# K projection in front of the output projection in a cross-attention kernel on one core

## The chip, the cores and the metric

The kernel runs on one core of one Trainium2 chip. The metric is the device time of one execution in microseconds (us), and lower is better. Three runs took 1128.15, 1130.78 and 1132.11 us (median 1130.78). A core has a matrix engine (TensorE, PE in the profile), a vector engine (VectorE, DVE), an activation engine (ScalarE, ACT), a general engine (GpSimd, POOL) and a queue that issues the DMAs (SyncE, SP). Each of them works through its own instructions in order; semaphores order them against each other.

## The reference

Eight batch items of 128 tokens with width 512 go through cross-attention with 32 heads of 128, a quantised feed-forward layer, a channel attention with a small convolution, and a routed low-rank layer. The change lies in the attention:

```python
x = _rmsnorm(hidden_states, ln_weight)
h_q = (x @ w_q.T).reshape(b, lq, H, DH)
h_k = (key_value_states @ w_k.T).reshape(b, lk, H, DH)
h_v = (key_value_states @ w_v.T).reshape(b, lk, H, DH)
score = jnp.einsum('bqhd,bkhd->bhqk', h_q, h_k) + position_bias[None]
score = jax.nn.softmax(jnp.where(m, score, -jnp.inf), axis=-1)
attn = jnp.einsum('bhqk,bkhd->bqhd', score, h_v).reshape(b, lq, H * DH)
out = attn @ w_out.T
```

All of it is in float32. A product of two float32 matrices is made of three matmuls: each operand is split into a rounded part ("hi") and the rest ("lo"), and lo by hi, hi by lo and hi by hi are added up.

## The kernel before

**Steps.** The attention is 64 steps, numbered n: 32 heads for batch items 0 to 3 (the first half), then the same heads for items 4 to 7 (the second half). Two steps are a pair, and a pair's odd step also prepares the V weights of a later pair. In the first half VectorE does rounds of a top-k search (`pick_round`) between its attention work; in the second half each step also quantises a slice of the feed-forward weights (`rows=True`).

**TensorE in step n**, in this order (L1273 to L1332): the scores of head n into `pS` (L1282); `queries(n + 1)`, twelve matmuls into `pX0`; `outputs(n - 1)`, twelve matmuls that add attention times W_out into the four banks `oacc`; `keys(n + 1)`, twelve matmuls into `pX1`; the transposes of the probabilities (`pS<-ident,prob`, L1303), which wait for `s_norm_done`; half of `values` of the next pair (24 smaller matmuls); in the second half two small products for the weight slice; then probabilities times V into `pT` (L1331).

**ScalarE in step n** (L624 to L659): four exponentials, the copy of the queries out of `pX0`, `hi("q", n + 2)`, `hi("o", n)`, in the second half the rounding `g_q`, `hi("k", n + 2)`, the copy of the values, in odd steps `value_high`, in the second half two copies (`gu_row`, `wguT`) that count `s_g_out`, then `aT_hi` from `pT`. `hi` rounds a weight tile `raw_*` into `w*_hi`, and first waits until TensorE has finished with the old one: for "o" until `outputs(n - 1)` is done (`s_o_done`), for "k" until `keys(n + 1)` is done.

**GpSimd in step n** (L502 to L513): the masked bias, then `lo("q", n + 2)`, `lo("o", n)`, `lo("k", n + 2)`, in odd steps `lo("v", m + 2)`; each waits for its `hi`.

**SyncE in step n** (L393 to L411): bias n+1, W_q and W_k of n+2, in the second half a slice for the feed-forward weights, W_o of n+1, and in odd steps W_v. There is one buffer `raw_*` of each kind, so a load waits for the `lo` that read the one before: the load of `raw_o` for step n+1 waits for `lo("o", n)`. The load of `raw_v` is issued behind it.

**VectorE in step n** (L891 to L970): `score` (pS plus bias), `neg_max`, in the second half the slice's scale, the pick rounds, the product of `prob` and `row_inv` (L935, sets `s_norm_done`), the copies `k_sb` and `pT_sb`, more pick rounds, then `aT_lo`, which waits for `aT_hi`. The next step's `score` stands behind `aT_lo`.

Of the kernel before, what the change touches and what calls it, by code (L numbers as in the profile page):

```python
# [26 lines left out]
H = 32  # L27
# [22 lines left out]
def layers_kernel(nc, x, cT, mask, bias, ln_w, wq, wk, wv, wo, w_gate, w_up, w_down,  # L50
# [9 lines left out]
    def sem(name):  # L60
        return ctx.enter_context(nc.semaphore(name))

    with ctx:
# [177 lines left out]
        s_g_out = sem("g_out")  # L241
# [73 lines left out]
        def unless_last(n):  # L315

            return not isinstance(n, int) or n < STEPS
# [15 lines left out]
        def later(n):  # L333

            return not isinstance(n, int) or n > 0
# [879 lines left out]
        def _(pe):  # L1215
# [9 lines left out]
            def tr(dst, src, ident):  # L1225
                return mm(dst, src, ident, is_transpose=True, start=True, stop=True)  # L1226
# [13 lines left out]
            def project(dst, c, src, half):  # L1240
                for kt in range(KT):
                    w = tuple(w[c][:, kt * P:(kt + 1) * P] for w in (w_hi, w_lo))
                    last = three(dst, w, tuple(s[half][:, kt, :] for s in src), start=kt == 0, stop=kt == KT - 1)
                return last

            def queries(n, half):
                pe.wait_ge(s_w_lo["q"], n + 1)
                project(pX0[:], "q", (xT_hi, xT_lo), half).then_inc(s_q_proj, 1)

            def keys(n, half):  # L1250
                pe.wait_ge(s_w_lo["k"], n + 1)
                project(pX1[:], "k", (cT_hi, cT_lo), half).then_inc(s_k_proj, 1)

            def values(part, half):

                for i in range(2):
                    b = 2 * part + i
                    for kt in range(KT):
                        c = tuple(t[half][:, kt, b * S:(b + 1) * S] for t in (cT_hi, cT_lo))
                        w = tuple(w["v"][:, kt * 2 * DH:(kt + 1) * 2 * DH] for w in (w_hi, w_lo))  # L1260
                        last = three(pX0[:, i * 2 * DH:(i + 1) * 2 * DH], c, w, start=kt == 0, stop=kt == KT - 1)
                last.then_inc(s_v_proj, 1)

            def outputs(n, start=False):
                pe.wait_ge(s_a_lo, n + 1)
                pe.wait_ge(s_w_lo["o"], n + 1)
                for b in range(HB):
                    cols = slice(b * S, (b + 1) * S)
                    last = three(oacc[b][:], (aT_hi[:, cols], aT_lo[:, cols]), (w_hi["o"][:], w_lo["o"][:]),
                                 start=start, stop=False, lint=True)  # L1270
                last.then_inc(s_o_done, 1)

            def pair(m, half, parity, rows=False):  # L1273
                for odd in range(2):
                    n = 2 * m + odd
                    pe.wait_ge(s_q, n + 1)
                    pe.wait_ge(s_k, n + 1)
                    if later(n):
                        pe.wait_ge(s_pT, n)
                    for b in range(HB):  # L1280
                        cols = slice(b * S, (b + 1) * S)
                        last = mm(pS[:, cols], q_sb[:, cols], k_sb[:, cols], start=True, stop=True)  # L1282
                    last.then_inc(s_s_done, 1)
                    next_half = (n + 1) // H if isinstance(n, int) else half
                    if unless_last(n + 1):
                        if isinstance(n, int) and n + 1 == H:
                            pe.wait_ge(s_xT_lo, B)

                        pe.wait_ge(s_v, n + 2 if not isinstance(n, int) else min(n + 2, STEPS))
                        queries(n + 1, next_half)  # L1290
                    if later(n):
                        if isinstance(n, int) and n == H + 1:
                            pe.wait_ge(s_x1_done, 1)
                        if isinstance(n, int) and n == 1:
                            pe.wait_ge(s_xw, B)
                        outputs(n - 1, start=isinstance(n, int) and n % H == 1)
                    if unless_last(n + 1):
                        if rows and not (isinstance(n, int) and n == H):
                            pe.wait_ge(s_g_out, n - H)
                        keys(n + 1, next_half)  # L1300
                    pe.wait_ge(s_norm_done, n + 1)
                    for b in range(HB):
                        last = tr(pS[:, b * S:(b + 1) * S], prob[:, b, :], ident[:])  # L1303
                    last.then_inc(s_p_trans, 1)
                    if unless_last(n + 2 if odd else n + 3):

                        if isinstance(m, int) and m + 1 == H // 2:
                            pe.wait_ge(s_cT_lo, 2 * KT)
                        pe.wait_ge(s_q, n + 2)
                        pe.wait_ge(s_w_lo["v"], m + 2)  # L1310
                        values(odd, (m + 1) // (H // 2) if isinstance(m, int) else half)
                    if rows:

                        pe.wait_ge(s_g_diag, n - H + 1)

                        if isinstance(n, int) and n + 1 == STEPS:
                            pe.wait_ge(s_g_out, n - H)
                        else:
                            pe.wait_ge(s_k, n + 2)
                        mm(pX1[:, 0:FR], ones[0:FR, :], f_diag[0:FR, 0:FR], start=True, stop=True)  # L1320
                        pe.wait_ge(s_g_q, n - H + 1)
                        for kt in range(KT):
                            last = tr(g_trans_bank[:, kt * FR:(kt + 1) * FR], g_q[0:FR, kt * P:(kt + 1) * P],
                                      ident_b[0:FR, 0:FR])
                        last.then_inc(s_g_trans, 1)
                    pe.wait_ge(s_pT, n + 1)
                    pe.wait_ge(s_v, 2 * m + 2)
                    for b in range(HB):
                        cols = slice(b * S, (b + 1) * S)
                        heads = slice(odd * DH, (odd + 1) * DH)  # L1330
                        last = mm(pT[:, cols], v_sb[parity][:, b, heads], pT_sb[:, cols], start=True, stop=True)  # L1331
                    last.then_inc(s_a_done, 1)  # L1332
# [11 lines left out]
            for m in range(2):  # L1344
                pair(m, 0, m % 2)
            with pe.Fori(1, H // 4 - 1) as u:
                for j in range(2):
                    pair(2 * u + j, 0, j)
            for m in range(H // 2 - 2, H // 2):
                pair(m, 0, m % 2)  # L1350
# [229 lines left out]
```

## Time and profile before

| | |
|---|---|
| Median of three runs | 1130.78 us |
| Profiled execution, own time | 1128.72 us |
| Its span | 1127.0 us |
| Mean granted TensorE clock | 0.96 |
| Busy share PE, PEld, DVE, ACT, POOL | 89%, 76%, 62%, 45%, 44% |
| DMA | 87.22 MB, mean 77 GB/s |

The shares are means over all stages. The attention fills about 57 to 925 us of the span and the rest is what stands before and behind it, so the stage has to be read by itself, in windows and in the order of time. Matmuls overlap: a matmul of 512 columns shows 0.39 us, and the next one starts 0.23 us after it.

### The profile page before, as it was taken

Reading aid. Unit: us, or ns where it says so; the run is one execution under the profiler, and the core shown is the slowest. Engines: PE = TensorE matmul, PEld = TensorE weight load, DVE = VectorE, ACT = ScalarE, POOL = GpSimd, SP = SyncE. Lnnn points to the kernel's source line nnn. Section 1 sums busy time; section 2 is a strip of 40 time slices with the busy share of each in tenths; the row PEclk is TensorE's granted clock in tenths of the full one; section 3 lists DMA queues with packets and bytes.
Section 4 is the critical chain, followed back from the end, with each engine's and each line's share of the span. In section 5 each row is a group of like instructions: output and inputs, shape, how many; then the busy total and the mean of one; then the engine's idle time right before and its main releaser. Section 6 shows DMA issues by size and latency. Waiting matters only on the chain. (4 is left out here: it accounts for less than half of the span.)

```text
span 1127.0 us, 19424 instructions
## 1 busy us (share of the span) xinstructions
PE 1005.8 (89%) x6010; PEld 852.9 (76%) x6010; DVE 697.8 (62%) x1835; ACT 512.3 (45%) x1333; POOL 496.3 (44%) x370
## 2 busy tenths in 40 slices
PE   3798999999999999999999999999999976665455
PEld 2687888888888888888888888888888863332343
DVE  6676777777677677675444444444444479998375
ACT  2334344444434434444444444444444455767342
POOL 4544545454444455434444444444454412554200
PEclk8898999999999999999999999999999999999578
DMA  5222222222222223223222232223223100000001
GB/s 212 75 80 80 80 80 79 79 86 93 88 79 79 79 79 105 80 93 118 94 94 93 94 101 102 102 99 102 92 92 114 58 16 20 1 0 1 0 1 75
DMA packets 50325, 87.22 MB, mean 77 GB/s; under 512 B 6320, under 2 KB 15152, under 8 KB 50288
## 3 DMA queue, kind: packets, MB, share of 16 engines
q1 hardware_dynamic: 50288, 86.76, 23.3%
q8 instruction: 20, 0.33, 0.1%
q14 instruction: 17, 0.14, 0.0%
HBM read 84.64 MB, written 2.10 MB: 77 GB/s over the span
## 5 line engine op out<-in xcount | busy, mean ns | idle before, releaser
L632 ACT ACTIVATE prob<-score,neg_max 128x128 f32<-128x128 f32 x256 | 99.8, 391 | 140.6 <-DVE neg_max L899 140.5
L966 DVE TENSOR_TENSOR aT_lo<-pT,aT_hi 128x512 fp32r<-128x512 f32 x64 | 44.2, 691 | 179.2 <-ACT aT_hi L572 179.1
L1221 PE MATMUL pX<-wv_lo,cT_hi 128*128 128x256 f32 x512 | 151.4, 296 | 0.7 <-ACT v_sb L572 0.7
L464 POOL TENSOR_TENSOR wq_lo<-raw_q,wq_hi 128x512 fp32r<-128x512 f32 x64 | 92.2, 1441 | 130.7 <-ACT wq_hi L572 130.6
L1222 PE MATMUL pX<-wv_hi,cT_lo 128*128 128x256 f32 x512 | 145.9, 285 | 0.0
L1223 PE MATMUL pX<-wv_hi,cT_hi 128*128 128x256 f32 x512 | 145.9, 285 | 0.0
L472 POOL TENSOR_TENSOR b_mask<-b_raw,mask_add 128x512 f32<-128x512 f32 x64 | 74.7, 1168 | 151.2 <-DVE score L896 151.2
L464 POOL TENSOR_TENSOR wv_lo<-raw_v,wv_hi 128x1024 fp32r<-128x1024 f32 x32 | 76.9, 2402 | 109.0 <-ACT wv_hi L572 109.0
L572 ACT ACTIVATE v_sb<-pX 128x512 f32<-128x512 f32 x64 | 38.2, 597 | 175.7 <-PE pX L1223 175.7
L860 DVE COPY k_sb<-pX 128x512 f32<-128x512 f32 x64 | 44.1, 688 | 112.9 <-PE pX L1223 112.9
L1221 PE MATMUL pX<-xT_lo,wq_hi 128*128 128x512 f32 x256 | 107.3, 419 | 4.3 <-DVE xT_lo L848 4.3
L464 POOL TENSOR_TENSOR wk_lo<-raw_k,wk_hi 128x512 fp32r<-128x512 f32 x64 | 83.0, 1297 | 60.8 <-ACT wk_hi L572 60.4
L1221 PE MATMUL oacc<-wo_lo,aT_hi 128*128 128x512 f32 x256 | 100.8, 394 | 6.2 <-DVE aT_lo L966 6.0
L1223 PE MATMUL pX<-xT_hi,wq_hi 128*128 128x512 f32 x256 | 101.4, 396 | 0.0
L1222 PE MATMUL pX<-xT_hi,wq_lo 128*128 128x512 f32 x256 | 100.6, 393 | 0.0
L1222 PE MATMUL oacc<-wo_hi,aT_lo 128*128 128x512 f32 x256 | 100.2, 392 | 0.0
L1223 PE MATMUL oacc<-wo_hi,aT_hi 128*128 128x512 f32 x256 | 100.2, 391 | 0.0
L1221 PEld LDWEIGHTS pX<-wv_lo,cT_hi 128*128 128x128 f32 x512 | 99.3, 194 | 0.9 <-ACT v_sb L572 0.9
L1223 PE MATMUL pX<-cT_hi,wk_hi 128*128 128x512 f32 x256 | 99.8, 390 | 0.0
L1221 PE MATMUL pX<-cT_lo,wk_hi 128*128 128x512 f32 x256 | 99.8, 390 | 0.0
L1222 PE MATMUL pX<-cT_hi,wk_lo 128*128 128x512 f32 x256 | 99.8, 390 | 0.0
L1222 PEld LDWEIGHTS pX<-wv_hi,cT_lo 128*128 128x128 f32 x512 | 99.4, 194 | 0.0
(213 smaller groups left out, 2407.2 us busy)
## 6 DMA issues: line engine op xcount, KB each, us to landing
raw_q<-in_wq SPq DMA_DIRECT2D x64, 256.0 KB, 3.5
raw_k<-in_wk SPq DMA_DIRECT2D x64, 256.0 KB, 3.4
raw_v<-in_wv SPq DMA_DIRECT2D x32, 512.0 KB, 3.9
raw_o<-in_wo SPq DMA_DIRECT2D x64, 256.0 KB, 2.7
b_raw<-in_bias SPq DMA_DIRECT2D x64, 64.0 KB, 3.1
f_raw<-in_w_down SPq DMA_DIRECT2D x4, 688.0 KB, 6.5
g_raw<-in_w_gate SPq DMA_DIRECT2D x16, 172.0 KB
g_raw<-in_w_up SPq DMA_DIRECT2D x16, 172.0 KB
```

The costliest lines, as they stand in the source:

```text
L464: g.tensor_tensor(w_lo[c][:], w_raw[c][:], w_hi[c][:].bitcast(F32), ALU.subtract).then_inc(s_w_lo[c], 1)
L472: g.tensor_tensor(b_mask[:], b_raw[:].to_broadcast([P, HB, S]), mask_add[:, half * HB:(half + 1) * HB, :], ALU.add).then_inc(s_b_mask, 1)
L572: return a.activation(dst, src, ACT.Copy)
L632: e = a.activation(prob[:, b, :], score[:, b, :], ACT.Exp, bias=neg_max[:, b:b + 1], accum_out=row_sum[:, b:b + 1])
L860: v.tensor_copy(k_sb[:], pX1[:]).then_inc(s_k, 1)
L966: v.tensor_tensor(aT_lo[:], pT[:], aT_hi[:].bitcast(F32), ALU.subtract).then_inc(s_a_lo, 1)
L1221: mm(dst, lh, rl, start=start, stop=False, skip_group_check=lint)
L1222: mm(dst, ll, rh, start=False, stop=False, skip_group_check=lint)
L1223: return mm(dst, lh, rh, start=False, stop=stop, skip_group_check=lint)
```

## The change

In each step the twelve matmuls of `keys(n + 1)`, with their waits, are issued in front of those of `outputs(n - 1)`. No instruction is added or removed.

```diff
                         pe.wait_ge(s_v, n + 2 if not isinstance(n, int) else min(n + 2, STEPS))
                         queries(n + 1, next_half)
+                    if unless_last(n + 1):
+                        if rows and not (isinstance(n, int) and n == H):
+                            pe.wait_ge(s_g_out, n - H)
+                        keys(n + 1, next_half)
                     if later(n):
                         if isinstance(n, int) and n == H + 1:
                             pe.wait_ge(s_x1_done, 1)
                         if isinstance(n, int) and n == 1:
                             pe.wait_ge(s_xw, B)
                         outputs(n - 1, start=isinstance(n, int) and n % H == 1)
-                    if unless_last(n + 1):
-                        if rows and not (isinstance(n, int) and n == H):
-                            pe.wait_ge(s_g_out, n - H)
-                        keys(n + 1, next_half)
                     pe.wait_ge(s_norm_done, n + 1)
```

TensorE in a step of the first half before: from the last matmul of the queries (`pX0`) over the output projection (`oacc`) and the K projection (`pX1`) to the transposes.

```order
L1223 MATMUL pX0<-xT0_hi,wq_hi 128x512
L1221 MATMUL oacc0<-wo_lo,aT_hi 128x512 [waits wo_lo,a_lo]
L1222 MATMUL oacc0<-wo_hi,aT_lo 128x512
...
L1223 MATMUL oacc3<-wo_hi,aT_hi 128x512
L1221 MATMUL pX1<-cT0_lo,wk_hi 128x512 [waits wk_lo]
...
L1223 MATMUL pX1<-cT0_hi,wk_hi 128x512
L1226 MATMUL pS<-ident,prob 128x128 [waits norm_done]
```

The same place now:

```order
L1223 MATMUL pX0<-xT0_hi,wq_hi 128x512
L1221 MATMUL pX1<-cT0_lo,wk_hi 128x512 [waits wk_lo]
L1222 MATMUL pX1<-cT0_hi,wk_lo 128x512
...
L1223 MATMUL pX1<-cT0_hi,wk_hi 128x512
L1221 MATMUL oacc0<-wo_lo,aT_hi 128x512 [waits wo_lo,a_lo]
...
L1223 MATMUL oacc3<-wo_hi,aT_hi 128x512
L1226 MATMUL pS<-ident,prob 128x128 [waits norm_done]
```

The K projection moved twelve matmuls forward and the output projection twelve back; the transposes stay where they were.

TensorE in a step of the second half, at the seam in front of the transposes, before:

```order
L1223 MATMUL oacc3<-wo_hi,aT_hi 128x512
L1221 MATMUL pX1<-cT1_lo,wk_hi 128x512 [waits wk_lo,g_out]
L1222 MATMUL pX1<-cT1_hi,wk_lo 128x512
L1223 MATMUL pX1<-cT1_hi,wk_hi 128x512
...
L1226 MATMUL pS<-ident,prob 128x128 [waits norm_done]
```

And now, from the queries on:

```order
L1223 MATMUL pX0<-xT1_hi,wq_hi 128x512
L1221 MATMUL pX1<-cT1_lo,wk_hi 128x512 [waits wk_lo,g_out]
L1222 MATMUL pX1<-cT1_hi,wk_lo 128x512
L1223 MATMUL pX1<-cT1_hi,wk_hi 128x512
...
L1221 MATMUL oacc0<-wo_lo,aT_hi 128x512 [waits wo_lo,a_lo]
```

The wait for `g_out` (the copies of the step before) moved forward with the K projection. The order on VectorE, ScalarE, GpSimd and SyncE is the same before and after.

## Rows read from the trace of the kernel before

**Rows 1.** Stretches: length, busy time of the five, TensorE clock, DMA share, GB/s

```profile
200.00:300.00 100.00, 100.00 (x606) 88.88 (x605) 68.74 (x235) 41.51 (x109) 47.62 (x34) 1.00 0.27 88
600.00:700.00 100.00, 100.00 (x622) 88.90 (x621) 44.76 (x101) 48.47 (x133) 47.57 (x34) 1.00 0.27 88
```

**Rows 2.** TensorE's waits, whole span: total us, times, longest

```profile
PE pS L1226 <- DVE prob L935: 11.0, 7, 3.8
PE oacc L1221 <- DVE aT_lo L966: 6.0, 3, 2.3
```

**Rows 3.** Timeline, odd step 19: ScalarE (start, duration, engine, line, operation)

```profile
315.41 0.63 ACT L572 ACTIVATE wo_hi<-raw_o 128x512 fp32r<-128x512 f32 x1 [1.05 <-PE oacc L1223]
321.87 1.05 ACT L572 ACTIVATE wv_hi<-raw_v 128x1024 fp32r<-128x1024 f32 x1
```

**Rows 4.** Timeline, same step: GpSimd and the DMA issue of SyncE

```profile
316.12 1.29 POOL L464 TENSOR_TENSOR wo_lo<-raw_o,wo_hi 128x512 fp32r<-128x512 f32 x1 [0.39 <-ACT wo_hi L572]
318.94 1.29 POOL L464 TENSOR_TENSOR wk_lo<-raw_k,wk_hi 128x512 fp32r<-128x512 f32 x1 [1.52 <-ACT wk_hi L572]
318.03 0.33 SPq L361 DMA_DIRECT2D raw_v<-in_wv  x1
```

**Rows 5.** Timeline, TensorE in steps 19 and 20

```profile
315.15 0.39 PE L1221 MATMUL pX<-cT_lo,wk_hi 128*128 128x512 f32 x1
317.88 0.38 PE L1226 MATMUL pS<-ident,prob 128*128 128x128 f32 x2
325.73 0.39 PE L1221 MATMUL oacc<-wo_lo,aT_hi 128*128 128x512 f32 x1
331.18 0.27 PE L1226 MATMUL pS<-ident,prob 128*128 128x128 f32 x1
```

**Rows 6.** Timeline, VectorE in steps 19 and 20

```profile
323.44 0.69 DVE L966 TENSOR_TENSOR aT_lo<-pT,aT_hi 128x512 fp32r<-128x512 f32 x1 [2.11 <-ACT aT_hi L572]
328.40 1.72 DVE L935 TENSOR_TENSOR prob<-prob,row_inv 128x512 f32<-128x512 f32 x1
```

**Rows 7.** raw_v, issue to landing, over 120 to 480 us, then 480 to 870

```profile
DMA to landing us min/median/max: 3.3/3.6/4.5
DMA to landing us min/median/max: 3.7/4.1/6.3
```

**Rows 8.** Timeline, steps 23 and 24: a late landing, and the transposes behind

```profile
371.23 0.33 SPq L361 DMA_DIRECT2D raw_v<-in_wv  x1
375.85 1.06 ACT L572 ACTIVATE wv_hi<-raw_v 128x1024 fp32r<-128x1024 f32 x1 [0.66 <-DMA raw_v<-in_wv]
382.37 1.73 DVE L935 TENSOR_TENSOR prob<-prob,row_inv 128x512 f32<-128x512 f32 x1
384.40 0.27 PE L1226 MATMUL pS<-ident,prob 128*128 128x128 f32 x1
```

**Rows 9.** Timeline, TensorE's waits in steps 26, 2 and 33

```profile
411.98 0.33 PE L1226 MATMUL pS<-ident,prob 128*128 128x128 f32 x1 [0.82 <-DVE prob L935]
88.21 0.48 PE L1226 MATMUL pS<-ident,prob 128*128 128x128 f32 x1 [3.79 <-DVE prob L935]
518.25 0.50 PE L1221 MATMUL oacc<-wo_lo,aT_hi 128*128 128x512 f32 x1 [2.34 <-DVE aT_lo L966]
```

**Rows 10.** Timeline, second half, steps 41 and 42

```profile
619.89 0.33 SPq L361 DMA_DIRECT2D raw_v<-in_wv  x1
623.80 1.06 ACT L572 ACTIVATE wv_hi<-raw_v 128x1024 fp32r<-128x1024 f32 x1
630.43 0.69 DVE L935 TENSOR_TENSOR prob<-prob,row_inv 128x512 f32<-128x512 f32 x1
633.44 0.27 PE L1226 MATMUL pS<-ident,prob 128*128 128x128 f32 x1
```

**Rows 11.** Stretches around the idle times of steps 2 and 33, columns as in rows 1

```profile
80.00:90.00 10.00, 6.21 (x29) 5.12 (x28) 8.90 (x23) 3.69 (x12) 8.12 (x7) 0.84 0.00 1
510.00:520.00 10.00, 7.66 (x51) 6.51 (x50) 4.14 (x8) 4.25 (x8) 3.41 (x2) 1.00 0.60 208
```

## The prediction

> **What bounds the kernel now.** I read the stretches first. Over 200 to 300 us and over 600 to 700 us TensorE is busy for the whole 100 us at the full granted clock, VectorE for 69 and 45 us, the others for less than half [rows 1]. So in the attention the time is TensorE's own work, and what the others do costs nothing as long as they are ready in time. The list of TensorE's waits says how rarely they are not: transposes that wait for the softmax product L935, 11.0 us in 7 places, and output projections that wait for `aT_lo`, 6.0 us in 3 [rows 2]. A change of order on an engine that is full can give back no more than such waits. It can cost a lot where it makes somebody else late, so the question is whose work is released by the moved matmuls, and how much room they have.
>
> The timeline of one pair answers that. In odd step 19 the output projection ends where the K projection starts, at 315.15, and the transposes start at 317.88 [rows 5]. `wo_hi` starts 0.26 us after the output projection's end [rows 3], `wo_lo` at 316.12 takes 1.29 us [rows 4], SyncE then issues `raw_o`, and behind it `raw_v` at 318.03 [rows 4]. ScalarE reads `raw_v` at 321.87 (`wv_hi`) [rows 3]. Behind `wv_hi` in ScalarE's queue stands `aT_hi`, for that VectorE waits 2.11 us in front of `aT_lo` at 323.44 [rows 6], and behind `aT_lo` stands all of the next step's softmax, up to L935, which starts at 328.40 and ends at 330.12 [rows 6]. The transposes that need it start at 331.18 [rows 5]. The spare time of this chain is thus 1.06 us.
>
> That the chain is a real one shows where `raw_v` lands late by itself. In step 23 it is read at 375.85, 4.62 us after its issue instead of 3.84; L935 then ends at 384.10 and the transposes start at 384.40, so the spare time shrank from 1.06 to 0.30 us, as much as the read moved [rows 8]. Where GpSimd has one more operation in that place (steps 26 and 28), nothing is left and the transposes wait already [rows 9].
>
> **The change part by part.** It adds and removes no instruction; per step twelve K matmuls move 2.73 us forward (315.15 to 317.88, [rows 5]) and twelve output matmuls as much back. The transposes' place is the same.
>
> K forward. Its weights are ready: `wk_lo` for the next step ends at 320.23 [rows 4], and its matmuls would start where the output projection started, at 325.73 [rows 5], which leaves 5.5 us before and about 4.2 us when `wk_lo` has to go behind `wo_lo` (below). VectorE's `k_sb` comes earlier; it stands between L935 and `pT_sb`, off the tight part. In the second half the wait for the copies (`g_out`) moves forward with it; those copies stand behind `wv_hi` too, but the delay that they bring lies inside the one counted below, since output projection and transposes only follow later. Cost and gain: nothing.
>
> Outputs back, on `aT_lo`: one of the three waits of rows 2 lies in the loop's order, the 2.34 us of step 33 [rows 9]. It goes, since its data is needed 2.73 us later. The other two are at the end of the attention, where no K projection is left. Gain: at most 2.3 us.
>
> Outputs back, on `o_done`: `wo_hi` starts 2.73 us later, and with it `wo_lo`, `raw_o` and `raw_v`, all in odd steps. Four operations in a row on three queues, none with room in it: `wo_hi` waited for TensorE 1.05 us and `wo_lo` for `wo_hi` 0.39 us [rows 3, 4]. `raw_v` is issued at 320.76 instead of 318.03. A landing takes 3.6 us at the median of the first half [rows 7] and about 0.1 us until it is read, so `wv_hi` starts at 324.46, 2.59 us later than before. Everything behind moves as much, as rows 8 show, and against 1.06 us of room (about 0.05 us of it is the semaphore) the transposes of step 20 wait 2.59 - 1.01 = 1.6 us. In even steps no `wv_hi` stands in the queue, so the odd steps' softmax isn't late.
>
> Now the sum. There are 30 odd steps with such a load (n = 1 to 59).
> - First half, ordinary pairs, 11: 11 x 1.6 = 17.6 us.
> - Steps 26 and 28, with no room now: the whole 2.7 us each, 5.4.
> - Second half, 13 pairs: `raw_v` was issued at 619.89 and read at 623.80, L935 ended at 631.12 and the transposes started at 633.44, 2.32 us of room [rows 10]. Issued at 622.62, with the median landing of 4.1 us [rows 7] and 0.1, it is read at 626.82, 3.0 us later; 3.0 - 2.3 = 0.75 us each, 9.8.
> - Steps 2 and 4 have no room either (step 2 waits 3.79 us already [rows 9]): 2.5 each, 5.0.
> - The crossing of the halves: step 32 has no room either, 2.3; step 34 gets the late chain, less the wait that goes in step 33, 1.0 net. Together 3.3.
>
> Sum 41.1 us. The clock comes on top. In step 2 TensorE idled 3.79 us and the granted clock of that stretch of 10 us is 0.84, part of it at the lower of its levels (1.2 instead of 2.4 GHz); around the idle 2.34 us of step 33 it stayed at 1.00 [rows 9, 11]. Steps 2, 4, 26 and 28 would idle over 3 us now. The 0.16 of 10 us is 1.6 us of full speed lost; I take that for two of the four, 3 us, with 0 and 8 as ends. The Trainium skill warns of it in "TensorE: Matmul & The Clock Gate", section "HAM oscillation — how this bites in real kernels": a TensorE that waits for data again and again falls to half its clock each time and pays for warming up again. By that rule the loss would come in all 30 pairs; the trace shows both, a fall behind the longer idle time and none behind the shorter.
>
> From the profiled execution's own 1128.7 us: 1128.7 + 41.1 + 3 = 1172.8. The median of the runs is 2.1 us above it, within their spread of 4 us, so I say 1174.
>
> Bounds. With the shortest landings (3.3 us, [rows 7]) a first-half pair waits 1.3 and one of the second half, whose shortest is 3.7, 0.35: 14.3 + 4.6 + 12.7 for the other places = 31.6, or 1160. With the longest (4.5 us, taken for both halves) it is 2.5 and 1.15: 27.5 + 15 + 14 = 56.5, and 8 us of clock: 1193. A price below nothing is bounded by rows 2: 2.3 us, if nothing of the delay were seen.
>
> **The rivals.**
> *The clock falls in every pair.* The 30 waits leave TensorE idle for 0.7 to 3.7 us (step 2: some 6). If each brought a fall of the size in step 2 (1.6 us in that stretch, and as much again in the next), it would be 30 x 3.2 = 96 us instead of 3: about 1265. For it speaks step 2; against it that 2.34 us of idle time passed without a fall, and that most of the new waits are shorter [rows 9, 11]. Chance 0.05.
> *The delay is covered, and only the wait of step 33 goes (the other side).* The place is `aT_lo` in front of the output projection: the price is minus 2.3 us, 1126.4 on the profiled execution, and 1128.5 against the median. It decides if `wv_hi` comes no more than 1.0 us later, so if SyncE could issue `raw_v` without waiting for `wo_lo`, or if the landing shrank from 3.6 to 2.0 us. Against it: the load stands behind `raw_o` in the order of SyncE, and the shortest landing is 3.3 us. TensorE being full speaks for it only as long as nobody is late. Chance 0.05, most of it within 0.3% of before.
> *Only the first half pays.* If the second half's landings are as short as in step 41 (3.9 us with the read), its term falls to 13 x 0.4 = 5, and without loss of clock the time is 1165. It is inside the range. Chance 0.15, against 0.75 for the forecast.
>
> **How the numbers follow.** The forecast and the last rival make 0.90 and fill 1158 to 1193; I give 1158 to 1192 for 8 in 10, since the places without room (steps 2, 4, 26, 28, 32) are the least certain. 0.3% is 3.4 us, about what runs of this kernel can tell. Slower: 0.75 + 0.15 + 0.05 = 0.95, less 0.01 for what I have not seen: 0.94. Same 0.04, faster 0.02.
>
> **What would show it.** Right, if in odd steps `wo_hi` starts about 0.3 us after the start of the transposes, `raw_v` is issued 2.8 to 2.9 us after it, `wv_hi` starts at 6.4 to 7.5 us instead of 4.0 to 4.8, and if even steps show a wait "pS <- prob L935" of 1.3 to 2.5 us in the first half and 0.4 to 1.2 in the second, some 45 to 55 us in about 30 places instead of 11.0 in 7, while odd steps show none. Even steps would be 14.6 to 15 us long instead of 13.3. The wait of 2.34 us for `aT_lo` in step 33 should be gone. Wrong, if `raw_v` is issued where it was, if L935 ends before the last output matmul all the same, or if the waits fall on odd steps, which would mean that another chain (K's weights) is the late one. A granted clock below 1.00 in the middle of the attention outside steps 24 to 30 would speak for the first rival.

## The result, and the profile after

The changed kernel takes 1166.94 us (median of four runs, 1164.20 to 1169.50) against 1130.24 us for the kernel before in the same comparison: the ratio is 1.0325, with a 95% interval of 1.0294 to 1.0355. It is 36.7 us slower. The forecast was 1174 with a range of 1158 to 1192, by the mechanism that the runs show. Three terms of its sum were two to five times too large, and a part of that was made up by what it had put lower or at nothing.

The page of the changed kernel starts with the span, the busy shares and the TensorE clock in 40 slices:

```profile
span 1162.5 us, 19424 instructions
PE 1018.0 (88%) x6010; PEld 856.4 (74%) x6010; DVE 704.6 (61%) x1835; ACT 508.3 (44%) x1333; POOL 493.1 (42%) x370
PEclk8899899999999999999999999999999998989677
```

The instructions are as many as before and the span is 35.5 us longer. 23.3 us of that are more idle time of TensorE, and its busy time rose from 1005.8 us before to 1018.0, at a mean granted clock of 0.954 instead of 0.964. Its stretches, as in [rows 1] (length, busy times, clock, DMA share, GB/s):

```profile
200.00:300.00 100.00, 94.88 (x565) 83.04 (x565) 70.06 (x228) 39.73 (x106) 46.55 (x33) 1.00 0.25 79
600.00:700.00 100.00, 99.86 (x617) 87.58 (x616) 45.97 (x102) 48.42 (x135) 48.10 (x34) 1.00 0.27 88
```

TensorE was busy for all of both stretches before [rows 1]. Now it idles 5.1% of the first half's stretch, and hardly in the second half's. The list of its waits over the whole span, to be held against [rows 2]:

```profile
PE pS L1226 <- DVE prob L935: 34.9, 18, 5.9
PE oacc L1221 <- DVE aT_lo L966: 3.5, 2, 2.0
PE pX L1221 <- ACT wguT L572: 1.0, 2, 0.8
```

Transposes wait 34.9 us instead of 11.0, in 18 places. The prediction had named 45 to 55 us in about 30 places: in the second half nearly all waits are under 0.15 us, and this list begins there. The 2.34 us in front of the output projection of step 33 are gone, and the two waits at the end of the attention stayed. The third line is the moved wait for `g_out`, in steps 34 and 60. It adds nothing: in both steps the transposes start right behind L935 all the same, 0.05 to 0.06 us after its end.

Now the chain, in steps 17 and 18, for [rows 3 to 6]. First ScalarE, GpSimd and SyncE, then VectorE, then TensorE (start, duration, operation, idle time before it and its releaser):

```profile
306.02 0.63 ACT L572 ACTIVATE wo_hi<-raw_o 128x512 fp32r<-128x512 f32 x1 [3.78 <-PE oacc L1223]
306.73 1.30 POOL L464 TENSOR_TENSOR wo_lo<-raw_o,wo_hi 128x512 fp32r<-128x512 f32 x1 [3.12 <-ACT wo_hi L572]
308.63 0.33 SPq L361 DMA_DIRECT2D raw_v<-in_wv  x1
312.19 1.06 ACT L572 ACTIVATE wv_hi<-raw_v 128x1024 fp32r<-128x1024 f32 x1 [2.33 <-DMA raw_v<-in_wv]
313.77 0.69 DVE L966 TENSOR_TENSOR aT_lo<-pT,aT_hi 128x512 fp32r<-128x512 f32 x1 [4.27 <-ACT aT_hi L572]
318.71 1.71 DVE L935 TENSOR_TENSOR prob<-prob,row_inv 128x512 f32<-128x512 f32 x1
...
305.76 0.60 PE L1226 MATMUL pS<-ident,prob 128*128 128x128 f32 x4
320.47 0.33 PE L1226 MATMUL pS<-ident,prob 128*128 128x128 f32 x1 [1.25 <-DVE prob L935]
```

From the start of the transposes (305.76) it is 0.26 us to `wo_hi`, 2.87 to `raw_v`'s issue, 6.43 to its reading (before: 0.15 and 3.99, [rows 3 to 5]). ScalarE, which did not wait for this DMA in step 17 before, waits 2.33 us for it, and step 18 is 14.71 us long instead of 13.30.

In the second half, steps 41 and 42, for [rows 10]:

```profile
650.50 0.33 SPq L361 DMA_DIRECT2D raw_v<-in_wv  x1
654.16 1.06 ACT L572 ACTIVATE wv_hi<-raw_v 128x1024 fp32r<-128x1024 f32 x1 [2.45 <-DMA raw_v<-in_wv]
660.79 0.69 DVE L935 TENSOR_TENSOR prob<-prob,row_inv 128x512 f32<-128x512 f32 x1
661.54 0.33 PE L1226 MATMUL pS<-ident,prob 128*128 128x128 f32 x1
```

L935 ends at 661.48 and the transposes start 0.06 us later, so all 2.3 us of room are used, and 0.2 us more. Landings of `raw_v`, for [rows 7] (120 to 480 us, then 480 to 870):

```profile
DMA to landing us min/median/max: 3.3/3.4/4.3
DMA to landing us min/median/max: 3.5/3.5/4.3
```

### The profile page after: what moved, and what is told of

It is laid out like the page before. It is cut to its first block and busy times, and to the rows that moved or that the text cites. A ratio compares the mean times of both kernels' runs of the same rounds, so it can differ in the third digit from the quotient of the medians.

```text
span 1162.5 us, 19424 instructions
## 1 busy us (share of the span) xinstructions
PE 1018.0 (88%) x6010; PEld 856.4 (74%) x6010; DVE 704.6 (61%) x1835; ACT 508.3 (44%) x1333; POOL 493.1 (42%) x370
## 5 line engine op out<-in xcount | busy, mean ns | idle before, releaser
L464 POOL TENSOR_TENSOR wo_lo<-raw_o,wo_hi 128x512 fp32r<-128x512 f32 x64 | 86.9, 1358 | 104.7 <-ACT wo_hi L572 104.6
L572 ACT ACTIVATE wo_hi<-raw_o 128x512 fp32r<-128x512 f32 x64 | 40.4, 631 | 137.8 <-PE oacc L1223 137.7
L1223 PEld LDWEIGHTS pX<-wv_hi,cT_hi 128*128 128x128 f32 x512 | 100.5, 196 | 0.0
```

What stands on the lines that cost most here:

```text
L464: g.tensor_tensor(w_lo[c][:], w_raw[c][:], w_hi[c][:].bitcast(F32), ALU.subtract).then_inc(s_w_lo[c], 1)
L572: return a.activation(dst, src, ACT.Copy)
L1223: return mm(dst, lh, rh, start=False, stop=stop, skip_group_check=lint)
```

## The experiments

Theory A: `outputs` behind `keys` lets `wo_hi` start 2.7 us later; `wo_lo`, `raw_o` and, in SyncE's order, `raw_v` follow; `wv_hi` stands in front of `aT_hi` in ScalarE's queue, and `aT_lo` in front of the next softmax on VectorE. Rival B: the moved K projection costs by itself (its weights, the wait for `g_out`, GpSimd and VectorE in each other's way). Times of the kernel before, in the first set of four, have a median of 1129.59 us, in the second of three 1129.55.

**The load of W_v first.** The changed kernel, SyncE's order alone edited:

```diff
+                    if odd and unless_last(n + 3):
+                        load("v", m + 2, ...)
                     if unless_last(n + 1):
                         load("o", n + 1, head1)
-                    if odd and unless_last(n + 3):
-                        load("v", m + 2, ...)
```

> The changed kernel (K projection first), with one edit: in the odd steps SyncE issues raw_v in front of raw_o, so that it no longer stands behind a load that waits for wo_lo. Theory A (the loss is the late raw_v, which holds up wv_hi, aT_hi, aT_lo and the next softmax): wv_hi starts again right behind v_sb, 4.0 us after the start of the transposes instead of 6.4, aT_lo at 5.6 instead of 8.0, and the waits of the transposes in the middle of the first half are gone (steps of 13.30 us); the output projection's 2.3 us wait for aT_lo in step 33 is gone too. Time 1124 to 1131 us. Rival B (the moved K projection costs by itself, through wk_lo behind wo_lo, the moved wait for g_out, or GpSimd and VectorE in each other's way): little changes, 1155 to 1167 us.

Measured: 1123.52 us, ratio 0.9945 (0.9927 to 0.9963). All of the loss is gone and 6 us more, 0.5 us below the 1124 to 1131 expected. The chain in steps 15 to 17 (SyncE, ScalarE, VectorE, and TensorE's transposes of step 17) and the remaining waits of the attention:

```profile
280.75 0.33 SPq L361 DMA_DIRECT2D raw_v<-in_wv  x1
293.48 1.05 ACT L572 ACTIVATE wv_hi<-raw_v 128x1024 fp32r<-128x1024 f32 x1
295.05 0.69 DVE L966 TENSOR_TENSOR aT_lo<-pT,aT_hi 128x512 fp32r<-128x512 f32 x1 [1.83 <-ACT aT_hi L572]
289.48 0.27 PE L1226 MATMUL pS<-ident,prob 128*128 128x128 f32 x1
...
PE pS L1226 <- DVE prob L935: 8.3, 4, 3.5
PE oacc L1221 <- DVE aT_lo L966: 3.5, 2, 2.0
```

`raw_v` is issued 8.73 us ahead of the transposes and read 4.00 us behind them, with `wo_hi` as late as in the changed kernel. Rival B falls: with K first and every other consequence of it in place, nothing is lost. The 6 us come mostly from places where the kernel before waits or its clock is low: in the profiled attention step 34 is 2.6 us shorter than in the kernel before, steps 26 to 29 together 2.1 and steps 3 and 4 together 2.0, while step 1 is 1.5 us longer, by a fall of the clock.

**The same edit on the kernel before.**

> The kernel before (output projection first), with the same edit of SyncE alone. Theory A: the loads that landed late (read 4.6 to 4.8 us after the transposes' start) are early now, so steps 4, 26 and 28 lose most of their waits of 1 us and step 33 its 2.3 us: 2 to 5 us faster than before, 1125 to 1129 us, and within 2 us of the same edit on the changed kernel. Rival B: also about 1126, but then the same edit on the changed kernel stays 30 us above it.

Measured: 1128.17 us, ratio 0.9977 (0.9963 to 0.9991). It is faster than before by 0.2%, but 4.7 us slower than the same edit with K first, not within 2 us as expected. The intervals of the two ratios touch at 0.9963, but all six runs of the one (1123.20 to 1125.06 us) are faster than all twelve of the other (1125.70 to 1129.14), so once the load is early the kernel with K first is the faster one. In the profiled attention (from the transposes of step 0 to those of step 63) the two differ by 2.4 us (855.8 and 853.4), mostly in steps 4, 33, 26 and 28. The other 2.5 us of the two profiles lie outside the attention, where the kernels are the same (taken up below), so only about half of the difference is explained by the order. The 2.6 us in step 34 come here as well: that gain belongs to the early load and needs no move on TensorE.

**`wo_hi` late by itself.** The kernel before, TensorE untouched:

```diff
+                    if unless_last(n + 1):
+                        act.wait_ge(s_k_proj, n + 2)
                     hi("o", n, s_o_done)
```

> The kernel before, TensorE's order untouched; ScalarE's rounding of W_o (wo_hi) waits in addition until the K projection of the step is done, as it has to in the changed kernel by the order. Theory A: the whole loss comes back without any move on TensorE: wo_hi at 0.26 us after the transposes' start, raw_v issued at 2.9, wv_hi at 6.4, waits of about 1.3 us in the even steps of the first half; time 1162 to 1170 us. The wait for aT_lo in front of the output projection may come in addition, since aT_lo at 8.0 us is later than the 7.85 us at which the output projection starts. Rival B: the time stays at 1130 to 1135 us, since TensorE does what it did.

Measured: 1177.44 us, ratio 1.0402 (1.0373 to 1.0432). The loss comes without any move on TensorE, and 10 us more of it than in the changed kernel, above the 1162 to 1170 expected. TensorE's waits in the attention (up to 925 us), then the chain in step 17 (transposes at 303.37; the lines of the kernel are two higher here):

```profile
PE oacc L1223 <- DVE aT_lo L968: 31.1, 30, 2.0
PE pS L1228 <- DVE prob L937: 11.3, 16, 4.9
...
303.70 0.63 ACT L572 ACTIVATE wo_hi<-raw_o 128x512 fp32r<-128x512 f32 x1 [3.85 <-PE pX L1225]
306.31 0.33 SPq L361 DMA_DIRECT2D raw_v<-in_wv  x1
310.99 1.06 ACT L572 ACTIVATE wv_hi<-raw_v 128x1024 fp32r<-128x1024 f32 x1 [3.52 <-DMA raw_v<-in_wv]
```

The offsets are nearly those of the changed kernel, 0.33 and 2.94 us for 0.26 and 2.87. The output projection now stands first and meets the late `aT_lo` in all 30 pairs, in the second half too, where the softmax has room. So K first both makes the delay and shields TensorE from a part of it: of the 48 us that a late `wo_hi` costs with the old order, 37 are left with the new one.

**`wv_hi` behind `aT_hi`.** The changed kernel, ScalarE's order alone edited: `value_high(m + 2)` moves to the line after the copy into `aT_hi`.

> The changed kernel, with one edit on ScalarE: in odd steps the rounding of W_v (wv_hi) stands behind aT_hi instead of in front of it; raw_v is issued as late as in the changed kernel. Theory A (the link from raw_v to the softmax is ScalarE's queue): aT_lo starts at 5.0 us after the transposes' start, the second half has no waits. In the first half wv_lo (2.4 us on GpSimd) now falls beside the pick copies L924 and may hold them up by 1 to 2 us, as cT_lo does in step 26, so some wait of 0 to 1 us can stay there: 1126 to 1145 us. If instead the late raw_v harms in another way (wv_lo late for the values), it stays at 1155 or more.

Measured: 1126.71 us, ratio 0.9976 (0.9959 to 0.9994). `raw_v` is issued 2.87 us behind the transposes and read at 6.2 to 7.8, as late as in the changed kernel, yet `aT_lo` starts at 5.02 (5.43 in the second half) and the loss is gone. The link is ScalarE's queue. Where waits would be left I had the halves the wrong way round: the first half has none in its ordinary pairs, the second has mostly 0.2 to 0.5 us of room left and waits in five steps (34, 36, 54, 58 and 60). What takes the room is GpSimd, here in steps 41 and 42 (GpSimd, then VectorE):

```profile
621.37 2.40 POOL L464 TENSOR_TENSOR wv_lo<-raw_v,wv_hi 128x1024 fp32r<-128x1024 f32 x1 [4.04 <-ACT wv_hi L572]
623.73 1.16 POOL L472 TENSOR_TENSOR b_mask<-b_raw,mask_add 128x512 f32<-128x512 f32 x1
...
621.49 0.68 DVE L904 TENSOR_REDUCE f_s<-g_raw 86x1 f32<-86x512 f32 x1 [0.17 <-issue]
622.58 1.24 DVE L911 TENSOR_SCALAR f_diag<-ident,f_s 86x86 f32<-86x86 f32 x1
623.92 1.25 DVE L917 TENSOR_SCALAR g_mag<-g_raw,f_s 86x512 f32<-86x512 f32 x1
625.33 1.01 DVE L932 TENSOR_TENSOR row_inv<-row_inv,row_any 128x4 f32<-128x4 f32 x1
```

`wv_lo` now runs beside the softmax. L911 shows 1.24 us where it took 0.26 in the kernel before, L917 1.25 instead of 0.48, L932 1.01 instead of 0.16, while the reduction L904 keeps its 0.68.

**Both edits.**

> The changed kernel with both edits: raw_v issued in front of raw_o, and wv_hi behind aT_hi in ScalarE's queue. Theory A says that either edit alone takes raw_v out of the softmax's chain, so the second brings little: wv_hi at 5.5 us and aT_lo at 5.0 us after the transposes' start instead of 5.6, half a us less wait in steps 2 and 32, 1121 to 1125 us. Theory C (GpSimd's wv_lo now falls beside VectorE's next softmax and holds its copies and products up, as in the second half of the run with wv_hi behind aT_hi alone): nothing gained or 1 to 3 us lost against the early load alone, 1123 to 1127 us.

Measured: 1127.36 us, ratio 0.9999 (0.9983 to 1.0015). Theory C was right that the second edit does harm beside the first: 4 us more than the early load alone, where it had said 1 to 3. Two thirds of the harm are at one place. `wv_hi` now comes at 4.9 instead of 4.0 us, and GpSimd's `wv_lo` and the four `xT_lo` end 14.1 us behind the transposes of step 1 instead of 13.2. GpSimd's next operations then run beside the end of VectorE's softmax: L924 takes 2.01 us instead of 0.91 and L935 1.67 instead of 0.69. Step 2 is 18.99 us long instead of 16.97, and the clock falls for 6.8 us there instead of 3.4. Steps 4 and 32 add 0.6 us each.

**Second half only.** The load order of the first experiment, in the second half alone.

> The changed kernel; raw_v is issued in front of raw_o in the second half alone, and stays behind it in the first. This splits the loss by half. By the trace of the changed kernel the second half's 13 pairs lost 4.3 us and the late chain of steps 33 and 34 little: 1160 to 1163 us. By the prediction's own term (9.8 us for these pairs): 1155 to 1158 us. If the loss were even over the pairs it would be near 1147 us.

Measured: 1164.0 us, ratio 1.0293 (1.0258 to 1.0329), 1155.85 to 1173.44 over four runs. The first half holds nearly all of the loss. For the numbers of the two sides (1160 to 1163 and 1155 to 1158 us) the runs spread too far to decide; an even spread over the pairs (1147) is out. The spread itself tells something. The clock of the longest execution (1173.44 us) in three stretches is

```profile
280.00:320.00 40.00, 37.86 (x225) 33.74 (x224) 23.42 (x80) 12.60 (x32) 16.39 (x12) 0.96 0.25 80
430.00:490.00 60.00, 53.66 (x294) 47.22 (x293) 38.61 (x118) 20.62 (x56) 25.83 (x19) 0.91 0.27 86
600.00:900.00 300.00, 300.00 (x1888) 267.57 (x1887) 129.07 (x283) 139.81 (x379) 142.62 (x99) 1.00 0.31 95
```

In the first two stretches the clock falls three times, at waits of 2.14, 2.67 and 3.67 us (steps 16, 26 and 28), and it stays up at the waits of 1.2 to 1.9 us in the other steps from 6 to 24. So with waits in every pair the granted clock can drop in the middle of the attention, and without them, in the second half, TensorE is busy for 300 of 300 us at full clock.

**The early load, and `add_norm` early.** On top of the first experiment, VectorE does `add_norm` of steps 1 and 31 in front of its wait for `aT_hi`:

```diff
+                    if isinstance(n, int) and n in (1, H - 1):
+                        add_norm(n // (H - 1))
                     dve.wait_ge(s_a_hi, n + 1)
                     v.tensor_tensor(aT_lo[:], pT[:], aT_hi[:].bitcast(F32), ALU.subtract)
-                    if isinstance(n, int) and n in (1, H - 1):
-                        add_norm(n // (H - 1))
```

> The changed kernel with raw_v issued in front of raw_o, and in steps 1 and 31 VectorE does add_norm (four operations on xr that the attention doesn't need) in front of its wait for aT_hi instead of behind aT_lo. In step 1 VectorE idles there for about 2.5 us, and GpSimd isn't working beside it. If the remaining waits of steps 2 and 32 come from add_norm standing in front of the next softmax, step 2 gets 3 to 4 us shorter, the clock doesn't fall behind it, step 32 loses its 0.4 us: 1117 to 1121 us. If they come from the late aT_hi or from GpSimd, it stays at 1123 us.

Measured: 1122.53 us, ratio 0.9944 (0.9926 to 0.9963). VectorE in step 1, first with the early load alone, then with this edit:

```profile
77.08 0.69 DVE L966 TENSOR_TENSOR aT_lo<-pT,aT_hi 128x512 fp32r<-128x512 f32 x1 [1.83 <-ACT aT_hi L572]
77.87 5.75 DVE L855 TENSOR_SCALAR xr<-xr,keep,shift 128x512 f32<-128x512 f32 x4
```

```profile
75.47 4.01 DVE L855 TENSOR_SCALAR xr<-xr,keep,shift 128x512 f32<-128x512 f32 x4
79.39 0.68 DVE L968 TENSOR_TENSOR aT_lo<-pT,aT_hi 128x512 fp32r<-128x512 f32 x1
```

Step 2 gets 1.3 us shorter (15.67 for 16.97) and step 32 loses its 0.4 us, less than the 3 to 4 us expected: `wv_lo` on GpSimd starts at 76.77 here, so `add_norm` isn't alone after all. And the softmax is held up instead, beside GpSimd's work: L924, L932 and L935 of step 2 take 1.57, 0.90 and 1.68 us where they took 0.91, 0.16 and 0.69 with the early load alone. The clock still falls behind step 2. Against the early load alone the time can't be told apart (1122.53 and 1123.52 us, with nearly the same interval); the two are the fastest versions here.

## Why the prediction was right, and which terms were off

**The chain** came as forecast, link by link: `wo_hi` 0.26 us after the transposes' start, `raw_v` issued at 2.87, read at 6.3 to 7.3 in the first half, and waits for L935 in even steps of it (odd steps stay at 13.37 us). Cutting it at SyncE or at ScalarE removes the loss, making `wo_hi` late by itself brings it, there mostly as waits for `aT_lo`.

**The terms**, from the step lengths of the two profiled executions:

| term | forecast | measured |
|---|---|---|
| 11 ordinary pairs, first half | 17.6 | 17.4 |
| steps 26 and 28 | 5.4 | 1.1 |
| 13 pairs, second half | 9.8 | 4.3 |
| steps 2 and 4, waits | 5.0 | 4.7 |
| crossing, without clock | 3.3 | 0.7 |
| clock | 3 | 4.0 |
| outside the attention | 0 | 3.5 |
| sum | 44.1 | 35.7 |

The spans differ by 35.5 us; the remaining steps make up -0.2. The forecast was 8.4 us too high, and that is a balance: the first five terms are 12.9 us too high together, the last two 4.5 us too low. So the closeness of the total is in part luck. That the mechanism was right shows in the first term and in the chain.

*Second half.* The term mis-sized most is this one, by the landing of 4.1 us: here it was 3.5 at the median, and a wait is what is left of the delay after 2.3 us of room, so 0.6 us less landing turns 0.75 us of wait into 0.15 to 0.25. Where one landing was long (step 59, read at 7.65 us) the next step got 1.34 us longer. 0.8 of the 4.3 us are in the odd steps, each 13.77 us long instead of 13.70, which I had not counted. I had taken the landing time from the place where the kernel before issues `raw_v`. The three profiled executions that issue it 2.7 us later (this one, only `wo_hi` late, and `wv_hi` behind `aT_hi`) all have a median of 3.5 us in the second half, against 4.1 in the kernel before. Whether the median belongs to the place of the issue or to the execution stays open, with one profile of the earlier place. The long landings differ between executions: with only `wo_hi` late the second-half reads are spread from 6.3 to 7.6 us, here they lie at 6.4 to 6.6 but for step 59 and step 33. So this term depends on the execution too, and the profiled one was the fastest of the four runs of the changed kernel (1164.20 us). I took a median where room minus delay was near zero; the rival "only the first half pays" had the better number for this term, 5 us. Its total of 1165 is close by the same balance, since it too had 5.4 us for steps 26 and 28 and no clock.

*Steps 26 and 28.* The term, "the whole 2.7 us each", took L935 of before as fixed. It wasn't; VectorE, then GpSimd, in step 26 before and after:

```profile
406.27 2.18 DVE L924 TENSOR_SCALAR pick<-cT_raw 128x128 f32 x2 [0.19 <-issue]
410.23 1.69 DVE L935 TENSOR_TENSOR prob<-prob,row_inv 128x512 f32<-128x512 f32 x1
410.09 1.29 POOL L464 TENSOR_TENSOR wo_lo<-raw_o,wo_hi 128x512 fp32r<-128x512 f32 x1
```

```profile
429.08 2.16 DVE L924 TENSOR_SCALAR pick<-cT_raw 128x128 f32 x2 [0.19 <-issue]
433.03 0.69 DVE L935 TENSOR_TENSOR prob<-prob,row_inv 128x512 f32<-128x512 f32 x1
433.23 1.63 POOL L464 TENSOR_TENSOR wo_lo<-raw_o,wo_hi 128x512 fp32r<-128x512 f32 x1 [0.29 <-ACT wo_hi L572]
```

L935 started beside GpSimd's `wq_lo` and `wo_lo` before; now `wo_hi` comes later, GpSimd has a gap of 0.29 us, L935 starts in it, 0.20 us ahead of `wo_lo`, and takes 0.69 us. That is 1.0 us per step in favour of the change, by a narrow margin: in the profile of "second half only", with the same order in the first half and `raw_v` read 0.26 us later, L935 of step 26 starts 0.04 us behind `wo_lo` and takes 1.76 us. The landings of these two pairs were also 1.1 to 1.2 us shorter than in the profile before (3.3 and 3.4 us against 4.5).

*Crossing.* Step 32 got 3.0 us longer, step 33 2.2 (the clock took 2.6 us there, and the 0.5 us went by which step 33 was longer than an ordinary step before), and step 34 2.0 shorter. There the landing of 6.3 us of the profile before was 4.3.

*Clock.* I charged two new falls; two came, behind step 4 and behind step 32. The stretches with them, and TensorE's idle times in front:

```profile
120.00:130.00 10.00, 8.95 (x50) 8.73 (x51) 6.79 (x23) 1.20 (x2) 2.12 (x2) 0.67 0.29 87
520.00:530.00 10.00, 9.89 (x58) 9.59 (x59) 5.96 (x10) 4.13 (x8) 3.67 (x3) 0.70 0.29 103
...
121.05 0.47 PE L1226 MATMUL pS<-ident,prob 128*128 128x128 f32 x1 [3.41 <-DVE prob L935]
520.11 0.48 PE L1226 MATMUL pS<-ident,prob 128*128 128x128 f32 x1 [3.27 <-DVE prob L935]
```

A fall costs 2.5 us here; the 4.0 us of the table are 2.5 in step 5 and 2.6 in step 33, less 1.1 in step 3, behind whose start both kernels have a fall (granted clock over 90 to 95 us 0.63 before, 0.75 after), the changed kernel's more of it in TensorE's idle time. Behind waits of 1.2 to 2.1 us the clock stayed at 1.00 in this execution; the rival in which each pair falls was wrong as a rule. The length of the wait alone doesn't decide in these profiles: 2.34 us (kernel before) and 2.12 us (changed kernel) passed without a fall, and the 3.17 us in front of step 0's transposes passed in both kernels but not with the early load, while the clock fell at 2.11 us (`wv_hi` behind `aT_hi`), 2.14 us (second half only) and 2.22 us (`add_norm` early), and at 1.98 and 1.79 us with only `wo_hi` late. The Trainium skill's "TensorE: Matmul & The Clock Gate", section "HAM oscillation — how this bites in real kernels", describes a kernel in which TensorE waits for a DMA longer than it works, time after time. Here it works for most of each pair, and the prediction's reading that by that rule all 30 pairs would fall goes beyond the page. The traces bear it out for the longest waits and for some of the shorter ones.

*Outside the attention* nothing was forecast and 3.5 us were measured, 0.8 less ahead of it and 4.3 more behind. I don't put that down to the change: the same part is 267.4 us long in the kernel before, 270.9 in the changed one, 268.1 with the early load, 270.7 with the early load on the old order and 266.8 in the last experiment (273.0 at most, with the second half only), with nothing edited there and the clock at its lower level in other places each time. That it is the clock's place is argued, not tested.

**The gain** of 2.3 us at step 33 came, hidden under the loss, but not by the move alone. The landing there was 2.0 us shorter, and `aT_lo` started 9.05 us behind the transposes instead of 10.01; the early load brings the gain with the old order too. The other side failed as its condition said: the delay of `wv_hi` was 2.4 us, not below 1.0.

## What to carry to other kernels

Where the engine is busy all the time, as here, a swap of two pieces of work is decided by who waits for the piece that moves back, through all the queues behind it; here the path was TensorE, ScalarE, GpSimd, SyncE, a DMA, ScalarE again, VectorE, TensorE, and the harm came from a load that merely stood behind another one in an in-order queue. Put the load that needs the longest lead and has its buffer free first in such a queue: with that, the same swap turned from 3.3% slower to 0.55% faster. And where room minus delay is near zero, sum over the single steps with the range of landings and not with a median.

## What the runs showed of the hardware

Some VectorE operations that read SBUF and run beside a GpSimd `tensor_tensor` are held until it ends, by up to its whole length: the `tensor_tensor` with both inputs in SBUF (L935 0.69 or 1.7 us, L932 0.16 or 1.01) and the larger `tensor_scalar` (L911 0.26 or 1.24, and 2.39 beside `wv_lo`; L917 0.48 or 1.25; L924 0.21 or 0.92). Not held are reductions (L904, 0.68), the search operations L875 and L881 (0.29 and 0.28), and a `tensor_tensor` with one input in PSUM (`aT_lo`, 0.68 or 0.69 in every run). In the other order GpSimd is held: `wo_lo` took 1.63 us instead of 1.29 where L935 had started 0.20 us before it. The Trainium skill says in "GPSIMD Engine Reference", "1. Specifications", that GpSimd shares its SBUF interfaces with VectorE, with contention for instructions in a 2-port mode or with two SBUF inputs. The traces agree for two SBUF inputs; which mode L911, L917 and L924 ran in, they don't show. They add that a quarter of a microsecond between the queues can decide whether the price is paid (step 26 above).

I had not expected that an early issue can land later without harm: with the load in front, `raw_v` took 6.7 us at the median of the second half instead of 3.5 (4.9 instead of 3.4 in the first half), issued right behind the slice of the feed-forward weights, and was there in time in all pairs but the one of step 33, where ScalarE waited 1.2 us for it and TensorE didn't wait. That the load beside it makes it slow isn't tested.
